# The last layer of a four-layer convolution kernel: stacking copies replaced by products in 64 by 64 quarters of TensorE, edge terms computed once per four images

## The reference

```
X = jnp.fft.rfftn(x, axes=(-2, -1), norm='backward')
Xr, Xi = (jnp.real(X), jnp.imag(X))
Yr = _rconv(Xr, wr) - _rconv(Xi, wi) + b_real[:, None, None]
Yi = _rconv(Xr, wi) + _rconv(Xi, wr) + b_imag[:, None, None]
Y = lax.complex(Yr, Yi)
return jnp.fft.irfftn(Y, axes=(-2, -1), norm='backward')
...
x = x + _L3_conv_ref(_gn(x), L3_conv_w_real, L3_conv_w_imag, L3_conv_b_real, L3_conv_b_imag)
```

## Time and profile before

| | |
|---|---|
| runs | 6081.27 us median of 3 (6081.03 to 6088.88) |
| profiled execution, its own time | 6042.9 us |
| its span | 6040.5 us |
| mean granted TensorE clock | 0.962 |
| PE busy | 5074.1 us (84%) |
| DVE, ACT, POOL busy | 3721.6 (62%), 2505.5 (41%), 1998.3 (33%) |
| DMA traffic | 1309 MB, 217 GB/s |

### The profile page before, as it was taken

The page is one execution under the profiler, slowest core; times in us unless marked ns, Lnnn a source line. Parts: engine busy times, 40 slices in busy tenths (PEclk is TensorE's granted clock), DMA queues, the critical chain, the costliest instruction groups (busy, mean ns, idle before and its releaser), DMA issues. The chain is left out here.

```text
span 6040.5 us, 175866 instructions
## 1 busy us (share of the span) xinstructions
PE 5074.1 (84%) x77091; PEld 2766.5 (46%) x77091; DVE 3721.6 (62%) x6212; ACT 2505.5 (41%) x3849; POOL 1998.3 (33%) x1694
## 2 busy tenths in 40 slices
PE   3999999999999999999999666666777777778787
PEld 3444544544445455444445222224554444444454
DVE  3555555555524444444444999998996666666666
ACT  0222222222211111111111566668995777677675
POOL 0022222222222000000000566666772555555555
PEclk9999999999999999999999999998997888889898
DMA  6889989989877676776765666666995999999998
GB/s 159 217 232 253 256 248 253 254 232 270 224 211 201 180 202 180 190 195 179 200 183 161 223 209 211 211 199 234 312 312 158 220 216 217 210 212 220 215 220 189
DMA packets 470346, 1309.09 MB, mean 217 GB/s; under 512 B 56513, under 2 KB 57265, under 8 KB 450995
## 3 DMA queue, kind: packets, MB, share of 16 engines
q1 hardware_dynamic: 469582, 1297.85, 79.2%
HBM read 705.02 MB, written 455.08 MB: 192 GB/s over the span
## 5 line engine op out<-in xcount | busy, mean ns | idle before, releaser
L627 PE MATMUL c_p<-c_w,wc 128*32 128x512 f16 x55296 | 3035.5, 380 | 140.8 <-issue 104.2
L627 PEld LDWEIGHTS c_p<-c_w,wc 128*32 128x32 f16 x55296 | 1554.9, 97 | 1593.2 <-issue 201.0
L685 ACT ACTIVATE c_t<-c_p,cbias,cscale 128x512 f32<-128x512 f32 x512 | 398.2, 778 | 2623.8 <-PE c_p L627 2623.8
L1072 POOL TENSOR_TENSOR d_x<-d_e,d_x 128x512 f32<-128x512 f32 x340 | 460.5, 1364 | 1668.5 <-ACT d_e L1061 1660.3
L558 DVE TENSOR_TENSOR a_x<-c_t,a_x 128x512 f32<-128x512 f32 x256 | 176.3, 689 | 899.1 <-ACT c_t L685 888.6
L1036 PE MATMUL d_pp<-d_q,wq 128*128 128x512 f16 x2040 | 492.1, 383 | 254.7 <-DVE d_q L945 254.6
L548 DVE TENSOR_SCALAR c_y<-c_t 128x512 f16<-128x512 f32 x256 | 118.4, 462 | 689.0 <-ACT c_t L685 688.6
L1675 POOL TENSOR_TENSOR f_y<-f_y,f_x 128x512 f32<-128x512 f32 x256 | 330.2, 1290 | 598.0 <-ACT f_y L1646 597.5
L1677 POOL TENSOR_TENSOR f_t<-f_t 128x512 f32<-128x512 f32 (+1 forms) x260 | 429.6, 1652 | 103.6 <-DVE f_t L1450 87.1
L1552 PE MATMUL f_P<-f_z,f_wt 128*32 128x512 f16 x6144 | 448.6, 431 | 6.4 <-DVE f_t L1450 6.2
L1036 PEld LDWEIGHTS d_pp<-d_q,wq 128*128 128x128 f16 x2040 | 175.0, 98 | 571.5 <-DVE d_q L945 397.6
(11 more groups left out here) (235 smaller groups left out, 6274.1 us busy)
## 6 DMA issues: line engine op xcount, KB each, us to landing
c_w<-xs SPq DMA_DIRECT2D x144, 1056.0 KB, 12.4
c_w<-ys SPq DMA_DIRECT2D x144, 1056.0 KB, 12.0
d_x<-x SPq DMA_DIRECT2D x68, 1280.0 KB, 9.5
xs<-a_hl SPq DMA_DIRECT2D x72, 1056.0 KB, 9.7
ys<-c_y SPq DMA_DIRECT2D x576, 132.0 KB, 9.7
f_z<-f_hl SPq DMA_DIRECT2D x512, 130.0 KB, 6.9
f_z<-f_qh SPq DMA_DIRECT2D x512, 130.0 KB, 4.6
a_x<-in_x SPq DMA_DIRECT2D x256, 256.0 KB, 10.0
```

Of the source, the lines that this page charges most:

```text
L627: t = p.matmul(pg[32 * j:32 * j + 32, :], wu[:, blk, wl, var, di, :], buf[:, bk, xl * PW + PAD + dx:xl * PW + PAD + dx + NW], start=(di == ...
L685: s.activation(tt_[n % 3][:, :], pp[:, n % 4, :], ACT.Tanh, bias=cbias[:, blk:blk + 1], scale=cscale[:, blk:blk + 1]).then_inc(c_act, 1)
L1072: q.tensor_tensor(xw, te[n % 3][:, :], xw, ALU.add).then_inc(d_x, 1)
```

## The change

The stack and its DMAs are gone. TensorE multiplies x and q where they lie. A band is 128 partitions, and a product mixes only the 16 channels of one row, so its weights are zero except in blocks: rows 0 to 3 of the band need only partitions 0 to 63, rows 4 to 7 only 64 to 127. `half` issues two matmuls of 64 by 64, one for each half. The matmuls for x use the quarters (0, 0) and (64, 64) of the array, those for q the quarters (64, 0) and (0, 64), for which ACT's copy of the transposes swaps the two halves, so that q comes out with its halves exchanged. Each of the three products takes three passes (high by high, low by high, high by low) for x and for q, in two quarters: 3 x 3 x 2 x 2 = 36 matmuls of 512 columns per item. They are issued in three rounds. In round1 x goes to product 0 and q to product 1, in round2 the other way round, in round3 x of item i to product 2 and q of item i - 1 to its product 2, so that x and q at work together write different banks. The transposes stand between round1 and round2, half of the Hilbert products between round2 and round3, the other half behind. A counter `f_r` makes TensorE wait for its own earlier round before the next touches the same bank.

The edge terms are computed once for the four items of a band, 18 matmuls of 8 columns (one column set of the four images), and copied by ACT once in two instructions. The lag is 6 instead of 8. One buffer for the transposes instead of two frees a bank for a second buffer of product 2; `y0` and `t1` get a third buffer, `f_hl` a third, all from the space of the stack. On ACT the copy of the transposes comes ahead of `f_y`, on DVE the final sum two items late and ahead of the waves, and the waves of product 2 one item later than those of product 1. In layer 0 the tables have another layout of the same size; DVE makes them from two small sets instead of one set and a stack of POOL's, and POOL's four f32 operations per table go.

```diff
+                def table(ht, z):
+                    wx = wt[ht % 2][:, 384 * z:384 * z + 384].rearrange("p (l f r o) -> p l f r o", l=2, f=3, o=16)
+                    mt = wt[ht % 2][:, 768:1792].rearrange("p (l f r o) -> p l f r o", l=2, f=4, o=16)
+                    q.wait_ge(w_f, 8 * ht + 4 * z + 4)
+                    if ht >= 2 and z == 0:
                         q.wait_ge(w_td[ht % 2], 16 * (ht // 2))
                     for l in range(2):
+                        row = over(pt[:, 28:32], [[0, 3], [1, 4], [0, 16]])
+                        if z == 0:
+                            q.tensor_tensor(wx[:, l], over(mwh[0][:, l, :], [[16, 3], [0, 4], [1, 16]]), row, ALU.mult).then_inc(w_t, 1)
+                            continue
+                        q.tensor_tensor(wx[:, l], over(mwh[1][:, l, :], [[32, 3], [0, 4], [1, 16]]), row, ALU.mult).then_inc(w_t, 1)
+                        q.tensor_tensor(mt[:, l], over(mwh[1][:, l, 16:80], [[16, 4], [0, 8], [1, 16]]),
+                                        over(pt[:, 32:40], [[0, 4], [1, 8], [0, 16]]), ALU.mult).then_inc(w_t, 1)
...
-    NXF, LAG = 20, 8
+    NXF, LAG = 20, 6
...
-        hl = [sb(ctx, f"f_hl{i}", [128, 2, NB, 2, 260], F16) for i in range(2)]
+        hl = [sb(ctx, f"f_hl{i}", [128, 2, NB, 2, 256], F16) for i in range(3)]
         qh = [sb(ctx, f"f_qh{i}", [128, 2, NB, 2, 260], F16) for i in range(3)]
-        zz = [sb(ctx, f"f_z{i}", [128, 4, NB, 2, 260], F16) for i in range(2)]
...
+        kk = [sb(ctx, f"f_kk{i}", [128, NB, 8], F32) for i in range(2)]
+        y0 = [sb(ctx, f"f_y0{i}", [128, 2, 256], F32) for i in range(3)]
+        t1 = [sb(ctx, f"f_t1{i}", [128, 2, 256], F32) for i in range(3)]
...
-        tp = ps(ctx, "f_tp", [128, 2, 1024], F16)
+        tp = ps(ctx, "f_tp", [128, 1024], F16)
         qp = ps(ctx, "f_qp", [128, 2, 512])
-        P = ps(ctx, "f_P", [128, 3, 512])
+        P = ps(ctx, "f_P", [128, 4, 512])
...
                         low(z + 2)
+                    if 0 <= i - 2 < NI:
+                        finish(i - 2)
                     if 0 <= i < NI:
-                        waves(i)
+                        wave(i, 0)
                     if 0 <= i - 1 < NI:
-                        finish(i - 1)
+                        wave(i - 1, 1)
                     if 0 <= z - 1 < NI:
...
+                def correct(s_):
+                    ht, n = s_ - 1, 128 if s_ else 48
+                    qq, kv = qh[s_ % 3], kp[0:n, 0:6 * NB].rearrange("p (b c a) -> p c b a", c=3, a=2)
+                    m, f0 = (mt[ht % 3], 2) if s_ else (vm, 0)
+                    if s_:
                         p.wait_ge(f_wt[ht % 3], 16 * (ht // 3 + 1))
+                    p.wait_ge(f_ql, NB * s_ + 4)
+                    if s_:
+                        p.wait_ge(f_k, 2 * s_)
                     fst = True
+                    for f, c0, c1, o0, swap in ((5, 257, 259, 0, 0), (3, 256, 258, 1, 0), (2, 258, 259, 1, 1), (4, 259, 260, 1, 1)):
                         for l, wl in passes:
+                            edge = qq[0:n, l, :, 1::-1, c0:c1] if swap else qq[0:n, l, :, :, c0:c1]
+                            for c in range(c1 - c0):
+                                t = p.matmul(kv[:, o0 + c], m[0:n, wl, f - f0, 0:n], edge[:, :, :, c], start=fst, stop=False, skip_group_check=True)
+                                fst = False
                     t.then_inc(f_kp, 1)
...
+                def half(i, f, bank, l, wl, of_q, start, stop):
+                    ht = i // NB - 1
+                    w, r = (wq[ht % 3], place(i)[1]) if of_q else (wx[ht % 3], place(i)[0])
+                    for z in range(2):
+                        k0 = 64 * (1 - z if of_q else z)
+                        t = p.matmul(P[64 * z:64 * z + 64, bank, :].rearrange("p (a i) -> p a i", a=2), w[k0:k0 + 64, wl, f, :],
+                                     r[k0:k0 + 64, l, :, 0:256], start=start, stop=stop, tile_position=(k0, 64 * z))
+                    return t
...
+                def round1(i):
...
+                    p.wait_ge(f_w1, 2 * i)
+                    for z, (l, wl) in enumerate(passes):
+                        half(i, 0, 0, l, wl, False, False, False)
+                        t = half(i, 1, 1, l, wl, True, z == 0, False)
+                    t.then_inc(f_r, 1)
+                def round2(i):
+                    if i < NB:
+                        if i:
+                            p.wait_ge(f_w1, 2 * i)
+                        product(i, 1, 2).then_inc(f_p01, 1)
+                        return
+                    p.wait_ge(f_r, 2 * (i - NB) + 1)
+                    for z, (l, wl) in enumerate(passes):
+                        half(i, 1, 1, l, wl, False, False, z == 2)
+                        t = half(i, 0, 0, l, wl, True, False, z == 2)
+                    t.then_inc(f_p01, 1)
+                def round3(i):
+                    if i >= 2:
+                        p.wait_ge(f_w2, 2 * (i - 1))
+                    if i < NB:
+                        product(i, 2 + i % 2, 4).then_inc(f_p2, 1)
+                        return
+                    if i > NB:
+                        p.wait_ge(f_r, 2 * (i - NB))
+                    for z, (l, wl) in enumerate(passes):
+                        if i < NI:
+                            x_ = half(i, 2, 2 + i % 2, l, wl, False, z == 0, False)
+                            if z == 2:
+                                x_.then_inc(f_r, 1)
+                        if i > NB:
+                            q_ = half(i - 1, 2, 2 + (i - 1) % 2, l, wl, True, False, z == 2)
+                            if z == 2:
+                                q_.then_inc(f_p2, 1)
...
                     i = z - LAG
                     if 0 <= i < NI:
-                        correct(i)
-                        mix(i)
+                        round1(i)
                     if z < NI:
                         turn(z)
+                    if 0 <= i < NI:
+                        round2(i)
                     if 0 <= z - 1 < NI:
-                        hilbert(z - 1)
+                        hilbert(z - 1, 0)
+                    if 0 <= i <= NI:
+                        round3(i)
+                    if 0 <= z - 1 < NI:
+                        hilbert(z - 1, 1)
+                    if 0 <= i + 1 < NI and (i + 1) % NB == 0:
+                        correct((i + 1) // NB)
...
+                def correct(s_):
+                    n, k_ = 128 if s_ else 48, kk[s_ % 2]
+                    kv = kp[0:n, 0:6 * NB].rearrange("p (b c) -> p b c", c=6)
+                    s.wait_ge(f_kp, s_ + 1)
+                    if s_ >= 2:
+                        s.wait_ge(f_w2, 2 * NB * (s_ - 1))
+                        s.wait_ge(f_y0, 2 * NB * (s_ - 1))
+                    s.activation(k_[0:n, :, 0:6], kv, ACT.Copy).then_inc(f_k, 1)
+                    s.activation(k_[0:n, :, 6:8], kv[:, :, 2:4], ACT.Identity, scale=inv(NB * s_)).then_inc(f_k, 1)
...
-                    if 0 <= i < NI:
-                        correct(i)
                     if z + 3 < NI:
                         normal(z + 3)
                     if z + 2 < NI:
                         high(z + 2)
+                    if z < NI:
+                        turn(z)
                     if 0 <= i < NI:
                         mix(i)
-                    if z < NI:
-                        turn(z)
                     if 0 <= z - 1 < NI:
                         hilbert(z - 1)
+                    if 0 <= i + 1 < NI and (i + 1) % NB == 0:
+                        correct((i + 1) // NB)
...
+                def add_x(i):
+                    q.wait_ge(f_y0, 2 * (i + 1))
+                    q.tensor_tensor(y0[i % 3][:, :, :], y0[i % 3][:, :, :], par(xin[i % NXF][:, :]), ALU.add).then_inc(f_ax, 1)
+                def add_waves(i):
                     n = item(i)[2]
+                    q.wait_ge(f_w1, 2 * (i + 1))
+                    q.wait_ge(f_w2, 2 * (i + 1))
+                    q.tensor_tensor(t1[i % 3][0:n], t1[i % 3][0:n], t2[i % 2][0:n], ALU.add).then_inc(f_aw, 1)
                 q.wait_ge(f_v, mark["ready"])
+                for i in range(NI + 1):
+                    if NB <= i < NI:
+                        add_x(i)
+                    if i:
+                        add_waves(i - 1)
...
-                def stack(s_, src, p0, c):
-                    if s_ >= 2:
-                        e.wait_ge(f_pe, 3 * NB * (s_ - 1))
-                    for l in range(2):
-                        for j in range(4):
-                            e.dma_start(zz[s_ % 2][p0 + 32 * l:p0 + 32 * l + 32, j], src[32 * j:32 * j + 32, l]).then_inc(c, 16)
...
-                    if NB <= z < NI and z % NB == 3:
-                        e.wait_ge(f_lo, z + 1)
-                        stack(z // NB, hl[z // NB % 2], 0, zx[z // NB % 2])
-                    if 0 <= i - 1 < NI:
-                        store(i - 1)
-                    if NB <= z - 1 < NI and (z - 1) % NB == 3:
```

(59 more changed lines are left out.)

224 lines of the change are left out of this document (67 added, 157 removed).

## The result

The changed kernel takes 5876.31 us, median of 4 runs (5863.85 to 5881.26), against 6081.15 for the kernel before (6065.78 to 6088.88). The ratio is 0.966, 95% interval 0.964 to 0.969. The forecast was 5882 us.

The account below looks back on a forecast made before the run. The prediction took the stacking copies' DMA as the bound, 5.41 us per item. Start at 4642.4, 250 items at 4.68 us and the tail gave a span of 5841.8; plus 41 us, 5882 us, range 5835 to 5930.

Parts of the forecast that it names:

- The bound: Last layer: the stacking DMAs and the clock they cost set the period, 5.41 us per item against 3.83 of TensorE work.
- Longer work on TensorE: Last layer, per item: TensorE work rises from 3.83 to 4.68 us, 0.85 more, still 0.73 below the 5.41 period.
- Quarters side by side: The 36 quarter matmuls per item: four run at once like column strips, 9 lengths of 0.217, 1.96 us.
- the first rival: Quarters of the same columns do not run side by side: 18 lengths, item 6.64 us, total 6372 us; chance 0.08.
- The switches: TensorE tiling changes: three visits per item, each 0.093 us in and 0.106 back, 0.60 us against 0.20 before.
- Waits on TensorE: Waits for its own earlier rounds and the single transpose buffer cost nothing; uncovered, about 0.2 us of the item each.
- Other engines: ACT 3.84, DVE 3.49, POOL 2.91 us per item stay under 4.68; the loop through f_y also adds zero.
- The second rival: A loop through ACT, DVE and POOL becomes the bound: +0.3 us per item, 5957 us; chance 0.15.
- Edge terms: 18 merged matmuls per four images at 0.0267 us each: 0.12 us per item, 0.32 before.
- Lag and sum items: Start of last layer: lag 8 to 6 saves 6.0 us, merged edge terms of the four sum items 0.9 us.
- Layer 0's tables: Layer 0: POOL does 154 us less, but TensorE sets the pace, so nothing gained; 7 us at a tenth of its idling.
- The sum itself: Whole kernel: span ends at 5841.8 us, 199 less; adding the earlier 41 us between span and median gives 5882.

Follow-up runs that it names:

- e2: Changed kernel with the sixteen stacking copies per band put back as mere traffic to a scratch tile that nothing reads: 6018.19 us, ratio 0.991.
- e1: Kernel before, with the stacking copies of bands 2 to 63 and the waits for them left out: 5658.59 us, ratio 0.932.
- e7: Changed kernel without the q products of the 256 bands, 18 quarter matmuls per item instead of 36: 5867.65 us, ratio 0.963.
- e5: Changed kernel with round3 directly behind round2, two visits to the quarter tiling per item instead of three: 5808.34 us, ratio 0.956.
- e6: Changed kernel with rounds in the order 1, 3, 2 in one piece, one visit to the quarter tiling per item: 5762.25 us, ratio 0.948.
- e8: Changed kernel with round2 directly behind round1 and transposes behind both, so nothing covers the f_r wait: 5886.19 us, ratio 0.968.
- e3: Changed kernel with the edge terms computed per image, 72 matmuls of 2 columns per band instead of 18 of 8: 5967.07 us, ratio 0.981.
- e4: Changed kernel with the lag set back from 6 to 8: 5876.22 us, ratio 0.965.

## Why the prediction was right, point by point

- **The bound.** Right: the DMA queue, for the larger part by its bytes (e2), with the clock that went with it. Without the copies the kernel before loses 408 us and its clock is full (e1). The prediction's 5.41 - 3.83 = 1.58 us per item makes 403.
- **Longer work on TensorE.** Predicted +0.85 us per item, 217 us; measured 4.74 - 3.85 = 0.89 from the profiles and 203 to 218 us between e1 and the changed kernel. In the steady part it is 4.75 - 3.83 = 0.92, since e1 is not quite at TensorE's own pace; the 0.07 above the forecast are the switches, next but one.
- **Quarters side by side.** Right, by the price of column strips; the first rival is excluded by the rows after and by e7. The row halves agree with what the Trainium skill says of tiles that run in parallel (TensorEngine Tiling (Array Packing), Key Properties).
- **The switches.** 0.199 us per visit was taken from rows; measured 0.22 to 0.23 (e5, e6), since the first group of a visit is 0.024 us longer. That term was mis-sized by 0.07 us per item, some 16 us. The Trainium skill's page TensorE: Matmul & The Clock Gate (Single matmul latency) gives a lone matmul a fixed part of 0.166 us. As a price for each switch, which was the prediction's estimate and not the page's statement, it is too high here: the item would have been 5.08 us, and 4.74 came.
- **Waits on TensorE.** Right: covered at 0. e8 prices the `f_r` wait at 0.24 us if it is not.
- **Other engines.** Right: they add nothing at 4.74, nor at 4.29 (e6). At the 3.85 of e1 they are level with TensorE, with some 0.04 us of rest. The tightest loop went as reckoned, with `f_y` at its end 3.9 us into the item (5007.67 - 5003.78):

```profile
5006.65 1.02 ACT L1659 ACTIVATE f_y<-f_P,f_kk,sv 128x256 f32<-128x256 f32 x2
```

  The second rival is excluded.
- **Edge terms.** Right in price, 0.12 us per item; e3 confirms 0.026 us per matmul.
- **Lag and sum items.** Predicted 6.9 us; from the first transpose to the first band item it is 67.0 us before (4582.3 to 4649.3) and 56.4 after. e4 puts the lag at 5.7 of these 10.6 us; what makes the other 4.9, where 0.9 was forecast, stays open.
- **Layer 0's tables.** POOL is busy 268.06 instead of 353.08 us in the stretch, PE 1231.51 instead of 1234.11. Nothing gained, as predicted. That nothing is lost is not shown: the first transpose of the last layer stands at 4582.3 and 4584.2 us in the two profiles with the old tables (before, e1) and between 4575.4 and 4600.1 in the ten with the new ones, eight of them later than 4585. A loss of some 10 us lies within this.
- **The sum itself.** It said a span of 5841.8 us, and 5872.0 came: 30 us short. The items account for 23: 1208.4 us from first to last instead of 1185.3, of which 0.066 x 250 = 16 is the steady pace, 4 the four items with the longer constant terms that the sum left out, and 3 the last ones. The layers before took 10 us more in that execution than in the one profiled before, since the first transpose of the last layer stands at 4592.3 instead of 4582.3; in other executions of the same code it stood at 4575 to 4600, so this is scatter or a small cost of the new tables. The head was 4 us better. **The step that failed is the last one**: the 41 us between span and median of before were carried over as if they belonged to the kernel. They do not. The profiled execution of before was simply a fast one: its other runs, in all four jobs, took 6,055 to 6,107 us, and none was as low as 6042.9. For the changed kernel span and median are 4 us apart. The two errors, 37 us too much and 30 too little, nearly cancelled, so that 5882 against 5876 is this close is luck; by the steady item the mechanism was right to 0.07 of 4.75 us. By medians the gain is 205 us; the sum promised 199 and by spans 169 came.

## What to carry to other kernels

A hole in front of a consumer and a full DMA queue are worth what the consumer would need without them, and that can be read from the items between the holes: 3.83 us stood in the rows before anything was run. Spending 0.9 us of TensorE work per item to remove 1.6 us of waiting paid, but the order that came with it was not the best (e6 is 102 to 114 us faster): count how often an item changes the array's tiling, and let products in other banks cover the wait for one's own accumulation, rather than work of another tiling. A profiled execution is one draw; its distance to the median is not a constant of the kernel.
